# A state-space layer on one core: projection by whole tiles, the step size put in the decay exponent, and the turned x copied by ScalarE

## The chip, the cores and the metric

The kernel runs on one core of a Trainium2 chip. The metric is device time in microseconds (us). The kernel before took 762.07 us, the median of 3 runs (761.32 to 762.39).

## The reference

A decoder layer on x of 4 sequences by 256 tokens by 256 channels: a state-space mixer with 32 heads, a mixture chosen by token id, and a routed mixture of 16 experts, each followed by an addition and a layer norm. The change touches the mixer alone:

```python
proj = x @ Win.T                       # per head: x 64, z 64, B 128, C 128, dt 1
dt = softplus(dt_raw + dt_bias)
xc = silu(causal_conv(x_ssm, w_x)); Bc, Cc likewise       # 4 taps over time
decay = exp(dt * A)
h = dec_t * h + (dt_t * xc_t) * B_t ;  y = h @ C_t        # scan over 256 tokens
y = y * rsqrt(mean(y * y) + 1e-6) * silu(z);  out = y @ Wout.T
```

The kernel has no scan over h. With cum the running sum of dt*A, it takes for each head and sequence y[t] = sum over s <= t of (B_s . C_t) * exp(cum_t - cum_s) * dt_s * xc_s, which is matrix work.

## The kernel before, in words

The heads go in 16 pairs. A pair's projection has six tiles of 128 output channels (x of both heads, B and C of the first head, B and C of the second, z) by 1024 tokens. Everything is pipelined over steps: in step n, `front` is the projection and convolution of pair n, `mid` is the scores of pair q = n-1, `tail` is the end of pair r = n-2. `steps` (L197) runs step 0 (front), step 1 (front, mid), a loop with steps 2 to 15 (all three), step 16 (mid, tail) and step 17 (tail). Each engine has its own hand-written order of a step, and semaphores tie them together. The parts and the short names that the prediction uses:

- TensorE, `step` at L529. P0 to P11 are `project(j)` (L540): j // 2 is the tile, j % 2 the half of the tokens; six matmuls of 128x512 each (two halves of the channels by three products of split operands). P(j) writes PSUM bank j % 4, so it waits until VectorE has done the last tap of the same half two tiles earlier (`half_read`, L211). X0 and X1 are `x_to_tokens` (L532, four transposes each, into banks 4 and 5). S0 to S7 are `score(k)` (L556: sequence k // 2, head k % 2), into bank 4 + k % 2; S(k) waits until W(k-2) has emptied its bank, S0 and S1 until the turned x has been taken from it. M0 to M3 are `mix(p, b)` (L569), one for each sequence, into banks 6 and 7. MS0 and MS1 are `mean_square` (L585).
- Order on TensorE before: P0, M2, M3, MS0, X0, P1, X1, P2, P3, S0, P4, S1, MS1, P5, S2, P6, S3, P7, S4, P8, M0, M1, P9, S5 and so on: one unit of the score behind each projection group. M2, M3, MS0 and MS1 are pair r's, the rest of M, X and S pair q's.
- ScalarE, `step` at L857: z of pair q, then for j = 0 to 9 `copy(j)` (L871: PSUM to `conv`, scaled by the last tap's weight) and what `work[j]` lists: `silu` of tile 4, `square`, a table load (L914), `exp_decay(b)` (L880, the exponential for two units of decay), `rsqrt`; then a table load (L928) and `silu` of tiles 0 to 3.
- VectorE, `step` at L1077: `tap(m, i)` (L1096) adds the three other taps of tile m in place, with half taps and full taps by `TAPS_OF` (L33). t1, t2, t3a, t3b name the taps with shift 1, 2, 3 (first half), 3 (second half); each waits for the one that it builds on. Tile 0 is done in six half taps, tiles 1 to 4 in t1 (full), t2 (full), t3a, t3b. `between` places the other work among them: x_scaled (L1080, the turned x times dt, from banks 4 and 5 to `xs`), W0 to W7 = `weigh(k)` (L1089, score times decay), and `gate` (L1113).
- GpSimd, `step` at L375: `log_decay` (L346: cum_t - cum_s and the mask), `low_part` (L370, needed by MS), the split of the next weights (L335), `norm` (L362).
- SyncE (L230) loads weights two steps ahead and stores and rereads the running sum (L247 to L251).
- Once, within and behind step 0: ScalarE's softplus (L842), VectorE's `sum_dt` (L1053), TensorE's `turn_dt` (L505, 16 small transposes of dt and cum), VectorE's `take_dt` (L1070), for which TensorE and GpSimd wait.

The placing on VectorE before:

```python
between[0, 3] = [lambda: x_scaled(0)]
between[0, 5] = [lambda: x_scaled(1)]
for k, at_ in enumerate(((1, 0), (2, 0), (2, 1), (3, 0), (3, 1), (4, 0), (4, 1), (4, 3))):
    between[at_] = [lambda k=k: weigh(k)]
between[4, 2] = [lambda: gate(q, qp, 0)]
```

Of the kernel before, what the change touches and what calls it, by code (L numbers as in the profile page):

```python
# [15 lines left out]
ALU = mybir.AluOpType  # L16
# [3 lines left out]
P = 128  # L20
NB, T, D = 4, 256, 256
NT = NB * T
TB = NT // P
# [8 lines left out]

TAPS_OF = [[(slice(h, h + 1), s) for h in (0, 1) for s in (1, 2, 3)] if m == 0 else  # L33
           [(slice(0, 2), 1), (slice(0, 2), 2), (slice(0, 1), 3), (slice(1, 2), 3)] for m in range(NCONV)]
TAP_AT = [sum(len(t) for t in TAPS_OF[:m]) for m in range(NCONV + 1)]
# [18 lines left out]
PAD = -3.0e38  # L54
HIT = 3.0e38
LN_EPS = 1e-5
RMS_EPS = 1e-6


def build_layer(nc, xT, x, winT, wdtT, a_log, dt_bias, woutT, ids, ctxT, gateT, ebias, wsh, wgu, wdn, out):  # L60
# [4 lines left out]
    with ExitStack() as ctx:  # L65
# [16 lines left out]
        cum_b = sb("cum_b", [P, 2, 2, NT])  # L82
        dt_tok = sb("dt_tok", [P, TB, H])
        cum_tok = sb("cum_tok", [P, TB, H])
# [59 lines left out]
        def take(n):  # L144
# [31 lines left out]
                 "w_split u_done p_arg p_lo s_done xt_done y_done ms_done "  # L176
                 "a_copy a_z a_silu a_decay a_sq a_ln a_rs "
                 "v_tap v_xs v_m v_yz v_y "
                 "ld_wo ld_xt ld_late ld_rt ln_st "
# [51 lines left out]
        def _(sp):  # L231
# [14 lines left out]
            load_pair(1, 1)  # L246
            sp.wait_ge(S["d_dt"], 3)  # L247
            sp.dma_start(cum_dram, dt_cum).then_inc(S["st_cum"], 16)
# [16 lines left out]
            sp.wait_ge(S["s_done"], NPAIR * UNITS)  # L265
            sp.wait_ge(S["v_xs"], 2 * NPAIR)
            sp.wait_ge(S["xt_done"], 2 * NPAIR)
# [41 lines left out]
        def _(pool):  # L309
# [65 lines left out]
            def step(n, par, split_next, mid, tail, ahead):  # L375

                if mid:
                    log_decay(n - 1, 1 - par, 2)
                if tail:
                    low_part(n - 2, 1)  # L380
                if mid:
                    log_decay(n - 1, 1 - par, 3)
                if split_next:
                    split(n + 1, 1 - par)
                if tail:
                    norm(n - 2, par, 0)
                    norm(n - 2, par, 1)
                if mid:
                    low_part(n - 1, 0)
                if ahead:  # L390
                    log_decay(n, par, 0)
                    log_decay(n, par, 1)
# [102 lines left out]
        def _(pe):  # L495
# [9 lines left out]
            def turn_dt():  # L505

                pe.wait_ge(S["d_dt"], 3)
                pe.wait_ge(S["z_const"], 10)
                for i, src in enumerate((dt_l, dt_cum)):
                    for b in range(TB):  # L510
                        mm = pe.transpose(ps[:, 4 + i, b * H:(b + 1) * H], src[:, b * P:(b + 1) * P],
                                          ident[0:H, 0:H])
                mm.then_inc(S["s_dtT"], 1)
                pe.wait_ge(S["d_dtT"], 1)
# [14 lines left out]
            def step(n, par, front, mid, tail):  # L529
# [26 lines left out]
                def score(k):  # L556
                    b, h = k // 2, k % 2
                    c0, c1 = cols[b]
                    Bm, Cm = conv[:, qp, 1 + 2 * h, :], conv[:, qp, 2 + 2 * h, :]
                    ge(pe, S["a_silu"], q * NCONV + 3 + 2 * h)  # L560
                    if k < 2:
                        ge(pe, S["v_xs"], q * 2 + k + 1)
                    else:
                        ge(pe, S["v_m"], q * UNITS + k - 1)
                    pe.matmul(ps[:, 4 + k % 2, 0:T], Bm[:, c0:c0 + P], Cm[:, c0:c0 + T], start=True, stop=True)  # L565
                    pe.matmul(ps[:, 4 + k % 2, T:SC], Bm[:, c1:c1 + P], Cm[:, c1:c1 + P], start=True, stop=True  # L566
                              ).then_inc(S["s_done"], 1)

                def mix(p, b):  # L569
# [3 lines left out]
                    if b % 2 == 0:  # L573
                        ge(pe, S["v_xs"], p * 2 + 1 + g)
                        ge(pe, S["a_ln"], p * 2 - 1 + g)
# [16 lines left out]
                if front:  # L592
                    ge(pe, S["w_split"], n * 2 + 2)
                    if isinstance(n, int) and n == 0:
                        pe.wait_ge(S["d_x"], 2)
                for j in range(2 * NTILE):
                    if front:
                        project(j)
                    if tail and j == 0:
                        mix(r, 2)  # L600
                        mix(r, 3)
                        mean_square(r, 0)
                        if isinstance(n, int) and n == NPAIR + 1:
                            pe.wait_ge(S["a_z"], 2 * NPAIR)
                            out_project(0, 0, NPAIR - 1)
                    if mid and j < 2:
                        x_to_tokens(j)
                    if mid and 3 <= j < 3 + UNITS:
                        score(j - 3)
                    if mid and j == 8:  # L610
                        mix(q, 0)
                        mix(q, 1)
                    if tail and j == 4:
                        mean_square(r, 1)
# [218 lines left out]
        def _(act):  # L833
# [8 lines left out]
            def softplus(i):  # L842
# [10 lines left out]
                else:  # L853
                    act.wait_ge(S["a_dt"], 4)
                    act.activation(dt_ch, dt_e, ACT.Ln, bias=1.0).then_inc(S["a_dt"], 1)

            def step(n, par, front, mid, tail):  # L857
                q, qp, r = n - 1, 1 - par, n - 2
# [12 lines left out]
                def copy(j):  # L871
                    tile, hf = j // 2, j % 2
                    ge(act, S["u_done"], n * 12 + j + 1)
                    if j == 0 and not (isinstance(n, int) and n < 2):
                        ge(act, S["s_done"], n * UNITS - UNITS)
                    tap = KD * PW + tile * TAPS + TAPS - 1
                    act.activation(conv[:, par, tile, hf * 512:(hf + 1) * 512], ps[:, j % 4, :], ACT.Copy,  # L877
                                   scale=w_raw[:, par, tap:tap + 1]).then_inc(S["a_copy"], 1)

                def exp_decay(b):  # L880
# [24 lines left out]
                if isinstance(n, int) and n == 0:  # L905
                    work[0] += [lambda: softplus(0)]
                    work[1] += [lambda: softplus(1), lambda: softplus(2)]
                    work[2] += [lambda: softplus(3)]
                if mid:
                    work[0] += [lambda: silu(q, qp, 4)]  # L910
                if tail:
                    work[1] += [lambda: square(r, 1)]
                if mid or tail:
                    work[1] += [lambda: act.preload_act_table_set("natural_log_exp_and_others")]  # L914
                if mid:
                    for b, j in enumerate((2, 4, 6, 8)):
                        work[j] += [lambda b=b: exp_decay(b)]
                    work[8].append(lambda: square(q, 0))
                if tail:
                    work[3] += [lambda: rsqrt(r, 0)]  # L920
                    work[6] += [lambda: rsqrt(r, 1)]
                for j in range(2 * NTILE):
# [121 lines left out]
        def _(dve):  # L1044
# [8 lines left out]
            def sum_dt():  # L1053
# [8 lines left out]
                dve.wait_ge(S["a_dt"], 5)  # L1062
                link(dve.tensor_tensor(dt_l, dt_l, dt_ch, ALU.add))
                link(dve.tensor_scalar(dt_da, dt_l, head_c[:, 2:3], -1.0, ALU.mult, ALU.mult))
                for b in range(NB):
                    t = slice(b * T, (b + 1) * T)
                    ins = dve.tensor_tensor_scan(dt_cum[:, t], one[:, :].broadcast_to([H, T]), dt_da[:, t], 0.0, ALU.mult, ALU.add)
                link(ins)

            def take_dt():  # L1070
                dve.wait_ge(S["s_dtT"], 1)
                dve.tensor_copy(dt_tok[:, :, :], ps[:, 4, 0:TB * H].rearrange("p (b h) -> p b h", b=TB))
                dve.tensor_copy(cum_tok[:, :, :], ps[:, 5, 0:TB * H].rearrange("p (b h) -> p b h", b=TB)  # L1073
                                ).then_inc(S["d_dtT"], 1)
                dve.wait_ge(S["d_dtT"], 1)

            def step(n, par, front, mid, tail):  # L1077
                q, qp, r, rp = n - 1, 1 - par, n - 2, par

                def x_scaled(c):  # L1080

                    ge(dve, S["xt_done"], q * 2 + c + 1)
                    ge(dve, S["y_done"], q * UNITS)
                    dve.tensor_tensor(xs[:, 4 * c:4 * c + 4, :].rearrange("p b (h c) -> p b h c", h=2),  # L1084
                                      ps[:, 4 + c, :].rearrange("p (b h c) -> p b h c", b=4, h=2),
                                      dt_tok[:, 4 * c:4 * c + 4, bass.ds(q * 2, 2)].unsqueeze(3)
                                      .broadcast_to([P, 4, 2, HP]), ALU.mult).then_inc(S["v_xs"], 1)

# [33 lines left out]
                if mid:  # L1122
                    between[0, 3] = [lambda: x_scaled(0)]
                    between[0, 5] = [lambda: x_scaled(1)]
                    for k, at_ in enumerate(((1, 0), (2, 0), (2, 1), (3, 0), (3, 1), (4, 0), (4, 1), (4, 3))):
                        between[at_] = [lambda k=k: weigh(k)]
                    between[4, 2] = [lambda: gate(q, qp, 0)]
                if tail:
                    between[0, 4] = [lambda: gate(r, rp, 1)]
                if isinstance(n, int) and n == 0:  # L1130
                    between[1, 0] = [sum_dt]
                for m in range(NCONV):
                    for i in range(len(TAPS_OF[m])):
                        for f in between.get((m, i), []):
                            f()
                        if front:
                            tap(m, i)
            steps(dve, step, take_dt)

# [252 lines left out]
```

## Time and profile before

| what | value |
|---|---|
| median of 3 runs | 762.07 us |
| profiled execution | 762.01 us |
| its span | 760.3 us (1.7 us lie around it) |
| TensorE matmul busy | 676.9 us, 89% |
| VectorE busy | 522.8 us, 69% |
| GpSimd busy | 437.8 us, 58% |
| ScalarE busy | 430.1 us, 57% |

The mixer takes about the first two thirds of the span: step 1 begins at 41.78 us, the steps of the loop at 68.74 us and then every 29.12 us, step 16 at 475.77 us. Busy time counts instructions from start to end and lets neighbours overlap, so an engine can be the bound with less than 100%. The profile is best read as the order of one step of the loop on each engine, since the steps repeat to a few hundredths of a microsecond.

### The profile page before, as it was taken

The numbers are of one execution on the slowest core, as the hardware profiler recorded it, in microseconds if no ns is written. First come the engines' busy times: TensorE is split into PE (matmuls) and PEld (weight loads), VectorE is DVE, ScalarE is ACT, GpSimd is POOL, SyncE is SP. The second block draws the span as 40 slices with busy tenths as digits, with TensorE's granted clock in tenths as the row PEclk, the third lists the DMA queues.
The fourth block names the chain that finished last, engine by engine and source line by source line (L and its number), as shares of the span: only waits on it lengthen the run. The fifth ranks groups of instructions, "written<-read, shape, count | busy, mean of one in ns | idle before, by whom it ended". The sixth has DMA issues, their size and how long they took to land.

```text
span 760.3 us, 11331 instructions
## 1 busy us (share of the span) xinstructions
PE 676.9 (89%) x3376; PEld 521.3 (69%) x3376; DVE 522.8 (69%) x803; ACT 430.1 (57%) x701; POOL 437.8 (58%) x382
## 2 busy tenths in 40 slices
PE   6599999999999999999999999899999986999930
PEld 3477777777777777777777777688846864677720
DVE  5988988988989989989889889512337343222236
ACT  4366777787787687687777777721011242333321
POOL 4076887787787777878868864754000014733134
PEclk9899999999999999999999999999999998999975
DMA  3221121121111211211211200430092401333324
GB/s 141 117 87 54 56 98 42 55 86 50 57 51 61 81 42 57 95 42 55 97 42 55 97 0 0 141 110 1 1 339 75 111 21 28 93 99 99 79 72 128
DMA packets 19968, 57.41 MB, mean 76 GB/s; under 512 B 2998, under 2 KB 13110, under 8 KB 17206
## 3 DMA queue, kind: packets, MB, share of 16 engines
q1 hardware_dynamic: 17686, 50.92, 19.6%
q0 software_dynamic: 2256, 6.16, 3.3%
q8 instruction: 14, 0.23, 0.1%
q14 instruction: 12, 0.10, 0.0%
HBM read 50.78 MB, written 6.29 MB: 75 GB/s over the span
## 4 chain that ended last, share of the span: by engine, by line
PE 51%; DVE 23%; issue 12%; ACT 9%; POOL 2%; DMA 1%; DVEq 1%; ACTq 0%; SPq 0%; POOLq 0%
DVE conv L1109 18%; PE ps L551 13%; PE ps L524 7%; PE ps L579 6%; PE ps L745 5%; PE ps L671 4%; PE ps L645 4%; PE ps L785 4%; ACT conv L877 3%; DVE decay L1093 2%; POOL conv L489 2%; ACT decay L883 2%; ACT y_hi L888 1%; PE ps L763 1%; PE ps L565 1%
## 5 line engine op out<-in xcount | busy, mean ns | idle before, releaser
L1109 DVE SCALAR_TENSOR_TENSOR conv<-ps,w_raw,conv 128x506 f32<-128x506 f32 (+3 forms) x352 | 324.6, 935 | 48.2 <-ACT conv L877 44.6
L551 PE MATMUL ps<-x_hi,w_hi 128*128 128x512 f32 x384 | 166.1, 433 | 29.8 <-DVE conv L1109 27.2
L877 ACT ACTIVATE conv<-ps,w_raw 128x512 f32<-128x512 f32 x160 | 109.3, 684 | 109.4 <-PE ps L551 109.2
L551 PE MATMUL ps<-x_hi,w_lo 128*128 128x512 f32 x384 | 151.6, 395 | 0.0
L551 PE MATMUL ps<-x_lo,w_hi 128*128 128x512 f32 x384 | 151.1, 393 | 0.0
L353 POOL TENSOR_TENSOR decay<-cum_b,cum_tok 128x512 f32<-128x512 f32 (+1 forms) x128 | 103.3, 829 | 35.5 <-DVE cum_tok L1073 23.8
L551 PEld LDWEIGHTS ps<-x_hi,w_hi 128*128 128x128 f32 x384 | 72.7, 189 | 56.2 <-DVE conv L1109 41.7
L373 POOL TENSOR_TENSOR y_lo<-y_sq,y_hi 128x512 fp32r<-128x512 f32 x32 | 41.3, 1289 | 80.1 <-ACT y_sq L889 80.1
L359 POOL TENSOR_TENSOR decay<-decay,mask 128x512 f32<-128x512 f32 x64 | 82.7, 1292 | 5.0
L551 PEld LDWEIGHTS ps<-x_hi,w_lo 128*128 128x128 f32 x384 | 72.5, 189 | 16.8
L551 PEld LDWEIGHTS ps<-x_lo,w_hi 128*128 128x128 f32 x384 | 73.0, 190 | 10.1
L862 ACT ACTIVATE conv<-conv 128x1024 f32<-128x1024 f32 x80 | 79.4, 1049 | 0.2
L565 PE MATMUL ps<-conv 128*128 128x256 f32 x256 | 76.4, 380 | 2.0 <-DVE xs L1084 1.6
L1093 DVE TENSOR_TENSOR decay<-ps,decay 128x384 f32<-128x384 f32 x128 | 70.2, 549 | 7.4 <-ACT decay L883 4.9
L937 ACT ACTIVATE ln_v<-ln_m,eps_ln 128x1 f32<-128x1 f32 x24 | 7.1, 295 | 90.6 <-DVE ln_m L1159 90.6
L524 PE MATMUL ps<-late,y_all 128*128 128x256 f32 x256 | 56.7, 379 | 0.2 <-DVE xs L1148 0.2
L565 PEld LDWEIGHTS ps<-conv 128*128 128x128 f32 x256 | 47.5, 188 | 13.2 <-issue 2.5
L458 POOL DMA_INDIRECT xb<-x_scratch,y_all x31 | 30.0, 967 | 42.5 <-PE ps L721 37.5
L343 POOL TENSOR_TENSOR w_lo<-w_raw,w_hi 128x1536 fp32r<-128x1536 f32 x15 | 53.0, 3531 | 1.2
L883 ACT ACTIVATE decay<-decay 128x768 f32<-128x768 f32 x64 | 53.4, 836 | 0.0
L566 PEld LDWEIGHTS ps<-conv 128*128 128x128 f32 x256 | 48.5, 190 | 6.7
L524 PEld LDWEIGHTS ps<-late,y_all 128*128 128x128 f32 x256 | 48.2, 190 | 6.9 <-DVE xs L1148 0.6
(166 smaller groups left out, 1027.1 us busy)
## 6 DMA issues: line engine op xcount, KB each, us to landing
cum_b<-cum_scratch SPq DMA_DIRECT2D x16, 1024.0 KB, 4.7
w_raw<-in_winT SPq DMA_DIRECT2D x16, 778.0 KB, 4.4
y_all<-in_wgu SPq DMA_DIRECT2D x4, 1408.0 KB, 10.7
ys_scratch<-y_blk SPq DMA_DIRECT2D x31, 128.0 KB, 1.7
late<-in_wdn SPq DMA_DIRECT2D x2, 1408.0 KB
late<-in_woutT SPq DMA_DIRECT2D x1, 2048.0 KB, 8.2
y_all<-in_xT SPq DMA_DIRECT2D x1, 1024.0 KB, 4.9
conv<-in_x SPq DMA_DIRECT2D x1, 1024.0 KB, 5.5
```

What stands on the lines that cost most here:

```text
L343: pool.tensor_tensor(w_lo[:, par, :], raw, w_hi[:, par, :].bitcast(F32), ALU.subtract).then_inc(S["w_split"], 1)
L353: pool.tensor_tensor(decay[:, 2 * b:2 * b + 2, c:t], cum_b[:, qp, :, b * T + j * P:(b + 1) * T], cum_tok[:, 2 * b + j, bass.ds(q * 2, 2)]. ...
L359: pool.tensor_tensor(diag, diag, mask[:, :].unsqueeze(1).unsqueeze(1).broadcast_to([P, 2, 2, P]), ALU.add).then_inc(S["p_arg"], 1)
L524: mm = pe.matmul(ps[:, b % 2, 0:D], y_all[:, i, b * P:(b + 1) * P], wo_sb[:, i, :], start=(i == 0), stop=(i == NPAIR - 1))
L551: mm = pe.matmul(ps[:, j % 4, :], wp[:, par, w], xp[:, kk, t], start=(i == 0), stop=(i == 5))
L565: pe.matmul(ps[:, 4 + k % 2, 0:T], Bm[:, c0:c0 + P], Cm[:, c0:c0 + T], start=True, stop=True)
L566: pe.matmul(ps[:, 4 + k % 2, T:SC], Bm[:, c1:c1 + P], Cm[:, c1:c1 + P], start=True, stop=True).then_inc(S["s_done"], 1)
L862: act.activation(conv[:, pp, tile, :], conv[:, pp, tile, :], ACT.Silu).then_inc(S["a_silu"], 1)
L877: act.activation(conv[:, par, tile, hf * 512:(hf + 1) * 512], ps[:, j % 4, :], ACT.Copy, scale=w_raw[:, par, tap:tap + 1]).then_inc(S["a_c ...
L883: act.activation(d, d, ACT.Exp).then_inc(S["a_decay"], 1)
L1093: dve.tensor_tensor(decay[:, k, :], ps[:, 4 + k % 2, 0:SC], decay[:, k, :], ALU.mult).then_inc(S["v_m"], 1)
L1109: dve.scalar_tensor_tensor(out=o[:, :, s:], in0=u[:, :, 0:T - s], scalar=w_raw[:, par, c:c + 1], in1=o[:, :, s:], op0=ALU.mult, op1=ALU.ad ...
```

## The change

The step size moves into the exponent: exp(cum_t - cum_s) * dt_s becomes exp(cum_t - (cum_s - log dt_s)). Only the second term, cum - log dt, is turned to the token side; dt isn't. The turned x is then copied unscaled by ScalarE instead of multiplied by VectorE. Three small operations are added in step 0 (a maximum and a subtraction on VectorE, a logarithm on ScalarE). The orders of all four engines change with it.

```diff
-TAPS_OF = [[(slice(h, h + 1), s) for h in (0, 1) for s in (1, 2, 3)] if m == 0 else
-           [(slice(0, 2), 1), (slice(0, 2), 2), (slice(0, 1), 3), (slice(1, 2), 3)] for m in range(NCONV)]
+TAPS_OF = [[(slice(0, 2), 1), (slice(0, 2), 2), (slice(0, 1), 3), (slice(1, 2), 3)] for m in range(NCONV)]
...
-            sp.wait_ge(S["d_dt"], 3)
+            sp.wait_ge(S["d_dt"], 4)
...
-            sp.wait_ge(S["v_xs"], 2 * NPAIR)
+            sp.wait_ge(S["a_xs"], 2 * NPAIR)
...
                 if mid:
                     log_decay(n - 1, 1 - par, 2)
+                    log_decay(n - 1, 1 - par, 3)
                 if tail:
                     low_part(n - 2, 1)
-                if mid:
-                    log_decay(n - 1, 1 - par, 3)
...
-                pe.wait_ge(S["d_dt"], 3)
+                pe.wait_ge(S["d_dt"], 5)
                 pe.wait_ge(S["z_const"], 10)
-                for i, src in enumerate((dt_l, dt_cum)):
-                    for b in range(TB):
-                        mm = pe.transpose(ps[:, 4 + i, b * H:(b + 1) * H], src[:, b * P:(b + 1) * P],
-                                          ident[0:H, 0:H])
+                for b in range(TB):
+                    mm = pe.transpose(ps[:, 4, b * H:(b + 1) * H], dt_ch[:, b * P:(b + 1) * P], ident[0:H, 0:H])
...
-                for j in range(2 * NTILE):
+                for tile in range(NTILE):
                     if front:
-                        project(j)
-                    if tail and j == 0:
+                        project(2 * tile)
+                        project(2 * tile + 1)
+                    if tail and tile == 0:
                         mix(r, 2)
                         mix(r, 3)
                         mean_square(r, 0)
...
-                    if mid and j < 2:
-                        x_to_tokens(j)
-                    if mid and 3 <= j < 3 + UNITS:
-                        score(j - 3)
-                    if mid and j == 8:
+                    if mid and tile == 0:
+                        x_to_tokens(0)
+                        x_to_tokens(1)
+                    if mid and tile == 4:
                         mix(q, 0)
                         mix(q, 1)
-                    if tail and j == 4:
+                    if mid and 1 <= tile < 5:
+                        score(2 * tile - 2)
+                        score(2 * tile - 1)
+                    if tail and tile == 2:
                         mean_square(r, 1)
...
+            def log_dt():
+
+                act.wait_ge(S["d_dt"], 2)
+                act.activation(dt_ch, dt_e, ACT.Ln).then_inc(S["a_dt"], 1)
+
...
+                def take_x(c):
+                    ge(act, S["xt_done"], q * 2 + c + 1)
+                    ge(act, S["y_done"], q * UNITS)
+                    act.activation(xs[:, 4 * c:4 * c + 4, :], ps[:, 4 + c, :].rearrange("p (b c) -> p b c", b=4), ACT.Copy
+                                   ).then_inc(S["a_xs"], 1)
+
...
+                    work[4] += [log_dt]
                 if mid:
                     work[0] += [lambda: silu(q, qp, 4)]
-                if tail:
-                    work[1] += [lambda: square(r, 1)]
                 if mid or tail:
                     work[1] += [lambda: act.preload_act_table_set("natural_log_exp_and_others")]
                 if mid:
+                    work[2] += [lambda: take_x(0), lambda: take_x(1)]
+                if tail:
+                    work[3] += [lambda: square(r, 1), lambda: rsqrt(r, 0)]
+                if mid:
                     for b, j in enumerate((2, 4, 6, 8)):
                         work[j] += [lambda b=b: exp_decay(b)]
-                    work[8].append(lambda: square(q, 0))
+                    work[9].append(lambda: square(q, 0))
                 if tail:
-                    work[3] += [lambda: rsqrt(r, 0)]
-                    work[6] += [lambda: rsqrt(r, 1)]
+                    work[7] += [lambda: rsqrt(r, 1)]
...
                 link(dve.tensor_tensor(dt_l, dt_l, dt_ch, ALU.add))
+                link(dve.tensor_scalar(dt_e, dt_l, DT_MIN, None, ALU.max))
...
+            def less_log_dt():
+
+                dve.wait_ge(S["a_dt"], 6)
+                dve.tensor_tensor(dt_ch, dt_cum, dt_ch, ALU.subtract).then_inc(S["d_dt"], 1)
+
...
-                dve.tensor_copy(dt_tok[:, :, :], ps[:, 4, 0:TB * H].rearrange("p (b h) -> p b h", b=TB))
-                dve.tensor_copy(cum_tok[:, :, :], ps[:, 5, 0:TB * H].rearrange("p (b h) -> p b h", b=TB)
+                dve.tensor_copy(cum_tok[:, :, :], ps[:, 4, 0:TB * H].rearrange("p (b h) -> p b h", b=TB)
...
-                    between[0, 3] = [lambda: x_scaled(0)]
-                    between[0, 5] = [lambda: x_scaled(1)]
-                    for k, at_ in enumerate(((1, 0), (2, 0), (2, 1), (3, 0), (3, 1), (4, 0), (4, 1), (4, 3))):
-                        between[at_] = [lambda k=k: weigh(k)]
-                    between[4, 2] = [lambda: gate(q, qp, 0)]
+                    for m in (2, 3, 4):
+                        between[m, 0] = [lambda m=m: weigh(2 * m - 4), lambda m=m: weigh(2 * m - 3)]
+                    between[4, 3] = [lambda: weigh(6)]
                 if tail:
-                    between[0, 4] = [lambda: gate(r, rp, 1)]
+                    between[1, 2] = [lambda: gate(r, rp, 1)]
                 if isinstance(n, int) and n == 0:
                     between[1, 0] = [sum_dt]
+                    between[3, 1] = [less_log_dt]
...
+                if mid:
+                    weigh(7)
+                    gate(q, qp, 0)
```

`S["v_xs"]` is replaced by `S["a_xs"]` in the waits of S0, S1 and `mix`, and the tile `dt_tok` is gone.

## Rows read from the trace of the kernel before

**Rows 1.** Waits within one step of the loop: us in total, times, longest.

```profile
POOL y_lo L373 <- ACT y_sq L889: 5.1, 2, 3.4
...
PE ps L551 <- DVE conv L1109: 2.2, 3, 0.9
```

**Rows 2.** Timeline of TensorE, one step (start us, us, what, idle before).

```profile
243.62 0.50 PE L551 MATMUL ps<-x_hi,w_hi 128*128 128x512 f32 x1 [0.91 <-DVE conv L1109]
...
245.19 1.52 PE L579 MATMUL ps<-decay,xs 128*64 128x256 f32 x16
246.64 0.50 PE L588 MATMUL ps<-y_hi,mean_w 128*128 128x512 f32 x1
...
247.20 0.60 PE L536 MATMUL ps<-ident,conv 128*128 128x128 f32 x4
247.56 0.48 PE L551 MATMUL ps<-x_hi,w_hi 128*128 128x512 f32 x1
...
249.03 0.60 PE L536 MATMUL ps<-ident,conv 128*128 128x128 f32 x4
...
250.86 0.39 PE L551 MATMUL ps<-x_hi,w_hi 128*128 128x512 f32 x1
...
252.22 0.59 PE L565 MATMUL ps<-conv 128*128 128x256 f32 x2
...
252.79 0.47 PE L551 MATMUL ps<-x_hi,w_hi 128*128 128x512 f32 x1
...
272.75 0.50 PE L551 MATMUL ps<-x_hi,w_hi 128*128 128x512 f32 x1 [0.91 <-DVE conv L1109]
```

**Rows 3.** Timeline of ScalarE, the same step.

```profile
244.48 1.06 ACT L868 ACTIVATE z_gate<-ps 128x512 f32<-128x512 f32 x2
...
249.23 0.69 ACT L877 ACTIVATE conv<-ps,w_raw 128x512 f32<-128x512 f32 x1 [2.17 <-PE ps L551]
...
252.79 0.84 ACT L883 ACTIVATE decay<-decay 128x768 f32<-128x768 f32 x1
253.53 0.68 ACT L877 ACTIVATE conv<-ps,w_raw 128x512 f32<-128x512 f32 x1
```

**Rows 4.** Timeline of VectorE, the same step.

```profile
254.24 4.03 DVE L1109 SCALAR_TENSOR_TENSOR conv<-ps,w_raw,conv 128x1020 f32<-128x1020 f32 x4
258.19 0.55 DVE L1093 TENSOR_TENSOR decay<-ps,decay 128x384 f32<-128x384 f32 x1
258.65 1.27 DVE L1109 SCALAR_TENSOR_TENSOR conv<-ps,w_raw,conv 128x1020 f32<-128x1020 f32 x1
...
271.36 0.68 DVE L1117 TENSOR_TENSOR z_gate<-ps,z_gate 128x512 f32<-128x512 f32 x1
271.95 0.74 DVE L1109 SCALAR_TENSOR_TENSOR conv<-ps,w_raw,conv 128x506 f32<-128x506 f32 x1
```

**Rows 5.** Timeline of TensorE in step 16, where two scores follow each other.

```profile
485.46 0.67 PE L565 MATMUL ps<-conv 128*128 128x256 f32 x2 [0.43 <-DVE decay L1093]
...
486.18 0.60 PE L565 MATMUL ps<-conv 128*128 128x256 f32 x2
```

**Rows 6.** Timelines of VectorE and TensorE in and behind step 0.

```profile
19.74 1.21 DVE L1063 TENSOR_TENSOR y_all<-y_all 32x1024 f32<-32x1024 f32 x1 [0.63 <-ACT y_all L855]
20.99 0.74 DVE L1064 TENSOR_SCALAR y_all<-y_all,head_c 32x1024 f32<-32x1024 f32 x1
...
41.31 0.42 DVE L1073 COPY cum_tok<-ps 128x256 f32<-128x256 f32 x1
```

```profile
27.65 0.79 PE L551 MATMUL ps<-x_hi,w_hi 128*128 128x512 f32 x1 [6.84 <-DVE conv L1109]
```

**Rows 7.** Busy us (x instructions) of PE, PEld, DVE, ACT, POOL; clock; DMA; GB/s, by stretch.

```profile
27.60:31.20 3.60, 3.55 (x8) 2.81 (x9) 3.53 (x4) 0.58 (x1) 0.00 (x0) 0.50 0.99 416
...
626.20:630.00 3.80, 0.09 (x1) 0.00 (x0) 3.80 (x4) 0.56 (x2) 3.79 (x3) 0.82 0.02 4
630.00:632.00 2.00, 1.75 (x17) 1.35 (x18) 1.97 (x4) 0.00 (x0) 0.00 (x0) 0.50 0.00 0
```

More of the change, by code:

```diff
@@ L55 @@
 HIT = 3.0e38
+DT_MIN = 1.0e-30
 LN_EPS = 1e-5
@@ L82, in build_layer @@
         cum_b = sb("cum_b", [P, 2, 2, NT])
-        dt_tok = sb("dt_tok", [P, TB, H])
         cum_tok = sb("cum_tok", [P, TB, H])
@@ L176, in build_layer @@
                  "w_split u_done p_arg p_lo s_done xt_done y_done ms_done "
-                 "a_copy a_z a_silu a_decay a_sq a_ln a_rs "
-                 "v_tap v_xs v_m v_yz v_y "
+                 "a_copy a_z a_silu a_xs a_decay a_sq a_ln a_rs "
+                 "v_tap v_m v_yz v_y "
                  "ld_wo ld_xt ld_late ld_rt ln_st "
@@ L561, in score @@
                     if k < 2:
-                        ge(pe, S["v_xs"], q * 2 + k + 1)
+                        ge(pe, S["a_xs"], q * 2 + k + 1)
                     else:
@@ L573, in mix @@
                     if b % 2 == 0:
-                        ge(pe, S["v_xs"], p * 2 + 1 + g)
+                        ge(pe, S["a_xs"], p * 2 + 1 + g)
                         ge(pe, S["a_ln"], p * 2 - 1 + g)
@@ L1078, in step @@
                 q, qp, r, rp = n - 1, 1 - par, n - 2, par
[L1080 to L1087, printed above, removed]
                 def weigh(k):
```

## The prediction

> **What bounds it now.** The timeline of one step of the loop decides, since 14 of the 18 steps repeat it. From P0 to the next P0 it takes 272.75 - 243.62 = 29.13 us [rows 2]. TensorE works nearly throughout. The reader sees only three waits in it, all for VectorE's taps, 2.2 us together and the longest 0.9 us, at P0 [rows 1]. So TensorE would need some 27.0 us alone, and the rest is VectorE not having emptied a bank. VectorE in turn idles only at the head of the step, where it waits for ScalarE's copies; from t1 of tile 1 at 254.24 on [rows 4] it runs nearly without a gap to the t3a that lets P0 go (start 271.95, 0.74 long, end 272.69, P0 at 272.75, so a hand-over costs 0.06). Two cycles are thus nearly equal, and what counts is the order, not the busy sums.
>
> **The prices.** From start to start, TensorE: a projection group behind another one 252.22 - 250.86 = 1.36, behind something else 249.03 - 247.56 = 1.47; a mix pair 1.45 with 0.09 ahead of it; MS 0.56; X 0.36; a score 252.79 - 252.22 = 0.57 [rows 2]. New is a score straight behind another: the first then costs 486.18 - 485.46 = 0.72 [rows 5]. ScalarE: a copy starts 249.23 - 247.56 = 1.67 after its projection group did, 0.57 before what follows it; the exponential takes 0.74; copy start to tap start is 254.24 - 253.53 = 0.71 [rows 2 to 4]. VectorE: t1, t2, t3a, t3b in a row, 258.19 - 254.24 = 3.95, of which t1 and t2 cost 1.32 each since the next tap waits for their end (without that, 1.27 less an overlap of 0.09: 1.18); W 0.46, ended after 0.55; gate 0.59 [rows 4].
>
> **take_x** has no row of its own. Above: the copies with a scale, 0.57 apart. Below: the silu of z, the same size from PSUM without a per-partition operand, (1.06 - 0.58) = 0.48 apart [rows 3]. It is nearest to the latter; I take 0.49, and 0.57 for the upper end (+0.16 a step).
>
> **One step of the new order,** P0 at 0. TensorE: P0, P1 (2 x 1.36), mix pair (0.09 + 1.45), MS0 0.56, X0 and X1 0.72: P2 at 5.54. Its copy starts at 7.21. On ScalarE both take_x and an exponential now stand between copy(2) and copy(3): 0.57 + 2 x 0.49 + 0.74, so copy(3) goes at 9.50, though P3's result is there by 5.54 + 1.47 + 1.36 + 0.2 = 8.6, and t1 of tile 1 starts at 10.21. Before it was 254.24 - 243.62 = 10.62; so 0.4 us is gained here, in spite of the copies. (All that VectorE saves in tile 0, two x_scaled and two half taps made full ones, lies ahead of this point and only makes its idle time longer. I give it nothing. Its cover is that P2 comes late; if P2 came early it would be worth up to 1.5 us.)
>
> Tile 1 on VectorE with the gate in it: 3.95 + 0.59 - 0.14 = 4.40, W0 at 14.61. And here is the new wait. S2 stands behind P5, and needs W0, which now stands behind all taps of tile 1. TensorE has ended S0, S1, P4 and P5 by 5.54 + 2.83 + 1.29 + 2.83 = 12.5 and sits idle until 14.61 + 0.55 + 0.06 = 15.22, **2.7 us**, with P6 and P7 queued behind, which have long been free to go. Before, P5 stood ahead of S2 as well, but W0 stood ahead of tile 1, and P6 followed at once.
>
> From there: S2 0.72, S3 0.57, MS1 0.56, P6 and P7 2.72 give 19.79; W2 starts at 14.61 + 0.92 + 3.95 = 19.48 and frees S4 at 20.09 (0.3 idle); S4, S5 1.29; P8, P9 2.83; mix pair 1.54; S6, S7 1.29; P10, P11 2.83: **next P0 at 29.87**. VectorE's own chain gives t1 of tile 1 + 4.40 + two times 4.87 (pair of W and tile) + 0.92 + 1.32 + 1.32 + 0.74 + 0.06 = 28.7, or 29.0 with a wait for copy(7), and so is no longer last. So a step costs 29.87 - 29.13 = +0.75, **+10.5 us** for 14 steps. The three old waits, 2.2, are indeed gone; 3.0 of new ones stand in their place.
>
> **What is hidden.** ScalarE: square of pair q moves behind copy(9) and the mix pair, so its silus at the step's end and copy(0) come about 1.5 later (copy(0) before at 244.48 + 0.95 - 243.62 = 1.8 [rows 2, 3]); this only eats VectorE's idle time, because copy(2) at 7.21 waits for P2. The cover is thin: by the same walk the table load ahead of copy(2) ends only some 0.4 before it. If that is gone, each 0.1 us costs 0.1 a step. GpSimd: low_part(r, 1) is moved behind one more log_decay, but GpSimd waited 5.1 us a step for the two squares [rows 1], and MS1 now needs it only at 16.5. SyncE's store of the sum comes about 1.2 us later, well ahead of GpSimd, which waits for take_dt anyway. MS1, S6, S7 find their inputs ready.
>
> **Outside the loop.** Step 0: the maximum costs 0.78 (as the scaling, 0.74 long, and the 0.04 by which such linked operations lie apart, 20.99 - 19.74 - 1.21), the later t1 of tile 0 0.4, and less_log_dt 1.21 less 0.2 of hidden tap wait [rows 6]; VectorE is the chain here. Gone is one copy of 0.42 that overlapped its neighbour (the other, cum_tok, stays). Sum +1.8, bounds 1 and 2.5. The eight transposes gone lie beside the taps. Step 1 without a tail, walked alike: +0.4. Step 16 has no P0, so the 0.9 wait ahead of P0 that is in the old 29.13 was never paid there, and the new step has none to save: +0.9. Step 16 itself: S2 waits for gate(r, 1), which now comes behind take_x and exp: +1.5, an estimate, between 0 and 3. **Sum: 1.8 + 0.4 + 10.5 + 0.9 + 1.5 = 15.1**, on 762.0 of the profiled execution (the median of the runs is the same to 0.1): 777. Bounds: prices off by 0.3 us a step either way (take_x, hand-over of W to S, scores in pairs) are 4 us, the rest 3.
>
> **Rivals.**
> (a) *TensorE becomes the bound, faster.* Its sum without waits is 27.0 as before, so 14 x 2.2 are to be had, less the 4.6 outside: 736. It decides at W0: its start would have to be by 12.0, so t1 of tile 1 by 7.6, a microsecond before P3's result exists. For it speaks that VectorE's work falls by a good microsecond a step, and that all three old waits are for it. Against it the order of W0 and S2. 0.09.
> (b) *VectorE's chain stays last.* If scores in pairs and the hand-overs cost less, or TensorE's end of step is quicker, the step is 28.7 to 29.2: with the parts outside 761 to 768. 0.15, a good half of it within 0.2% of before.
> (c) *The clock falls.* The granted clock was 0.50 after TensorE's pause of 6.84 us [rows 6, 7] and after one of 3.8 us (0.82 in it, 0.50 behind) [rows 7]; in the loop with pauses up to 0.9 it held. The new pause is 2.7 us in every step, between the two. At 0.50, which is 1.2 GHz, 8 matmuls took 3.6 us, against 1.8: +1.7 a step if it falls in each, 777 + 24 = 801. The Trainium skill ("TensorE: Matmul & The Clock Gate", its table of advice) warns of idle gaps between bursts of matmuls in just this way; the rows agree for the long pauses and show nothing of one of 2.7. 0.08.
> (d) *It does not do what it says:* the copies on ScalarE delay nothing and copy(3) goes at 8.6 as if alone. Then t1 of tile 1 is 0.9 earlier, the step 29.0, the time 765. Within (b).
>
> **Numbers.** As walked 0.68 (770 to 785), (a) 0.09, (b) and (d) 0.15, (c) 0.08. The likeliest is 777. The range 764 to 788 takes in the first and most of (b), leaves out (a) and (c). Faster by over 0.2% (about what a measurement can tell, 1.5 us) 0.10, within it 0.08, slower 0.82.
>
> **What would show it.** In the step's timeline: S2's pair idle 2 to 3 us until W0, S4 a few tenths, no wait at P0, P6, P8; copy(3) behind two take_x of about 0.6 long and an exponential; step near 29.9. VectorE's idle before t1 of tile 0 grown to 4 us. I am wrong if S2 doesn't wait, if the step is under 29.1, or if the clock in the loop is under 1.00.

## The result, and the profile after

The changed kernel took 791.72 us (median of 4 runs, 790.65 to 794.89) against 762.22 before: a ratio of 1.0396, with a 95% interval of 1.0366 to 1.0427. It is slower by 29.5 us, where 15 were forecast. The profiled execution took 794.89 us with a span of 793.2; it is the longest of the four (mean granted clock 0.945, the others 0.954 to 0.956).

The busy part of its page:

```profile
PE 691.3 (87%) x3368; PEld 530.3 (67%) x3368; DVE 501.5 (63%) x740; ACT 443.5 (56%) x734; POOL 437.6 (55%) x382
```

VectorE's busy time fell by 21 us, as it should, and TensorE's rose by 14 although it does a few transposes less. In the trace of before a matmul of 128x512 takes 0.39 us in a row of them, 0.50 straight behind a pause [rows 2] and 0.79 at half clock [rows 6], so this line points at pauses or at the clock. The length of the steps points at the clock. Timeline of TensorE, the eight transposes (X0, X1) of four steps in a row (start us, us, what):

```profile
232.36 1.03 PE L532 MATMUL ps<-ident,conv 128*128 128x128 f32 x8
...
262.40 0.93 PE L532 MATMUL ps<-ident,conv 128*128 128x128 f32 x7
...
293.81 0.93 PE L532 MATMUL ps<-ident,conv 128*128 128x128 f32 x7
...
323.86 0.93 PE L532 MATMUL ps<-ident,conv 128*128 128x128 f32 x7
```

The steps alternate: 30.04, 31.41, 30.05 us, and so on over the whole loop; before, every step took 29.1 us [rows 2]. Waits in the long step that P0 begins at 257.58 (us in total, times, longest):

```profile
ACT conv L881 <- PE ps L547: 7.5, 3, 6.1
DVE conv L1117 <- ACT conv L881: 7.0, 3, 4.2
...
PE ps L561 <- DVE decay L1101: 2.4, 1, 2.4
```

The waits of TensorE for taps [rows 1] are gone. One for a weighing stands in their place, ahead of S2, and VectorE idles 4.2 us at the head of the step (3.8 in the short one before it). The timeline of TensorE shows S2 of two steps, with its pause:

```profile
242.84 0.70 PE L561 MATMUL ps<-conv 128*128 128x256 f32 x2 [2.38 <-DVE decay L1101]
...
272.88 1.10 PE L561 MATMUL ps<-conv 128*128 128x256 f32 x2 [2.39 <-DVE decay L1101]
```

Both pauses are 2.4 us, but behind the second the same two matmuls take 1.10 us instead of 0.70. The stretches behind the two pauses, and one at the start of step 1 and one in step 16 (busy us of PE, PEld, DVE, ACT, POOL, then granted clock, DMA share, GB/s):

```profile
242.80:246.00 3.20, 3.16 (x16) 2.77 (x17) 3.13 (x4) 0.00 (x0) 3.12 (x2) 1.00 0.00 0
272.80:276.30 3.50, 3.42 (x10) 2.91 (x11) 3.43 (x5) 0.00 (x0) 3.42 (x2) 0.54 0.00 0
44.07:47.40 3.33, 3.33 (x8) 2.61 (x9) 0.00 (x0) 0.58 (x1) 3.17 (x4) 0.54 0.68 222
509.60:518.70 9.10, 8.54 (x24) 7.06 (x25) 3.23 (x6) 6.55 (x11) 6.69 (x7) 0.50 0.20 62
```

At 2.4 GHz behind the one, near 1.2 GHz behind the other. So the added time of the loop is made of two things: a step that is 0.9 us longer at the full clock, and half clock behind the pause in every second step (steps 2, 4 and so on to 14), 1.35 us each.

**Where the 32.9 us of the profiled execution lie**, by equal points of both traces: 2.3 up to P0 of step 1 (44.07 against 41.78 us); 2.3 in step 1; 22.3 from there to X0 of step 16, of which seven steps with half clock are 9.3; 4.9 from X0 of step 16 to the first transposes of the output projection, where S0 waits 3.1 us for ScalarE and the clock is 0.50 behind it; 1.1 after that, which was not followed further. What half clock cost in steps 1 and 16 can be read from later runs. Experiments 7 (with 6) and 8 have the same order in step 1; the first had half clock at its start and took 26.70 us for it, the other had none and took 25.30: 1.4 of the 2.3. In step 16 the profiles of experiment 2 (even) and experiment 3 have the changed kernel's order, a pause of 2.8 us and granted clock 1.00 throughout, and they take 2.6 us less from X0 on, of which 0.3 is the shorter pause: 2.3 of the 4.9. Half clock is then some 13 us in all, and the rest, some 20 us, is the order at the full clock.

### The profile page after: what moved, and what is told of

It reads as the page before. It is cut to its first block, busy times and chain, and to the rows that moved or that the text cites. A ratio compares the mean times of both kernels' runs of the same rounds, so it can differ in the third digit from the quotient of the medians.

```text
span 793.2 us, 11229 instructions
## 1 busy us (share of the span) xinstructions
PE 691.3 (87%) x3368; PEld 530.3 (67%) x3368; DVE 501.5 (63%) x740; ACT 443.5 (56%) x734; POOL 437.6 (55%) x382
## 4 chain that ended last, share of the span: by engine, by line
PE 47%; issue 16%; DVE 15%; POOL 14%; ACT 6%; DMA 1%; POOLq 1%; DVEq 1%; SPq 0%; ACTq 0%
PE ps L547 10%; DVE conv L1117 9%; POOL decay L352 9%; PE ps L520 7%; PE ps L744 5%; PE ps L561 4%; PE ps L670 4%; PE ps L644 3%; PE ps L784 3%; PE ps L575 2%; DVE decay L1101 2%; PE ps L562 2%; ACT conv L881 2%; POOL conv L487 1%; POOL decay L358 1%
## 5 line engine op out<-in xcount | busy, mean ns | idle before, releaser
L1117 DVE SCALAR_TENSOR_TENSOR conv<-ps,w_raw,conv 128x1020 f32<-128x1020 f32 (+1 forms) x320 | 316.9, 1008 | 101.5 <-ACT conv L881 96.3
L547 PE MATMUL ps<-x_hi,w_hi 128*128 128x512 f32 x384 | 158.3, 412 | 11.4 <-DVE conv L1117 10.1
L561 PE MATMUL ps<-conv 128*128 128x256 f32 x256 | 90.7, 440 | 40.2 <-DVE decay L1101 36.6
L547 PEld LDWEIGHTS ps<-x_hi,w_hi 128*128 128x128 f32 x384 | 74.4, 194 | 27.2 <-DVE conv L1117 11.3
L367 POOL TENSOR_TENSOR y_all<-z_gate,y_all 128x512 f32 (+1 forms) x32 | 41.5, 1296 | 54.0 <-ACT y_all L906 54.0
L1101 DVE TENSOR_TENSOR decay<-ps,decay 128x384 f32<-128x384 f32 x128 | 66.3, 548 | 6.1 <-PE ps L562 6.0
L562 PE MATMUL ps<-conv 128*128 128x128 f32 x256 | 54.0, 296 | 0.0
L456 POOL DMA_INDIRECT xb<-x_scratch,y_all x31 | 30.1, 970 | 42.6 <-PE ps L720 37.6
```

Source lines behind the costliest of these rows:

```text
L367: pool.tensor_tensor(dst, z_gate[:, pp, h], y_rs[:, g, :], ALU.mult).then_inc(S["v_y"], 1)
L547: mm = pe.matmul(ps[:, j % 4, :], wp[:, par, w], xp[:, kk, t], start=(i == 0), stop=(i == 5))
L1101: dve.tensor_tensor(decay[:, k, :], ps[:, 4 + k % 2, 0:SC], decay[:, k, :], ALU.mult).then_inc(S["v_m"], 1)
L1117: dve.scalar_tensor_tensor(out=o[:, :, s:], in0=u[:, :, 0:T - s], scalar=w_raw[:, par, c:c + 1], in1=o[:, :, s:], op0=ALU.mult, op1=ALU.ad ...
```

## The experiments

Ratios are to the kernel before, run on the same chip in the same rounds; where microseconds of two jobs are compared, the ratio times 762.2 is used. The step lengths are from the profiles.

**1. The pause filled.** P5 is computed twice in each step with scores (same operands, same bank, same result; only the second tells the others that it is done).

```diff
                         project(2 * tile)
+                        if mid and 2 * tile + 1 in (5,):
+                            project(2 * tile + 1, filler=True)
                         project(2 * tile + 1)
```

> The changed kernel, with P5 computed twice in every step that has scores: six more matmuls of 1.37 us in the pause before S2, same result. Theory one (the clock): in the changed kernel steps alternate between 30.05 and 31.4 us because the granted clock falls after every second pause of 2.4 us. With the pause cut to about 1.1 us the clock stays at 1.00, every step takes 30.05, and the whole is some 10 to 12 us faster than the changed kernel, 780 to 783 us, although TensorE does more. Theory two (the long steps come from a wait that varies with the order of the loop's two steps, and the clock only follows it): steps go on alternating, and the time stays at 791 us. Theory three (TensorE itself is short of time): 1.37 us more a step, 810 us.

Measured: 781.20 us, ratio 1.0217 (1.0189 to 1.0246). Its timeline of TensorE and the stretch behind the pause:

```profile
257.82 1.04 PE L532 MATMUL ps<-ident,conv 128*128 128x128 f32 x8
...
268.30 0.70 PE L562 MATMUL ps<-conv 128*128 128x256 f32 x2 [1.03 <-DVE decay L1104]
...
287.89 1.04 PE L532 MATMUL ps<-ident,conv 128*128 128x128 f32 x8
```

```profile
268.30:271.80 3.50, 3.50 (x18) 3.03 (x19) 3.43 (x4) 0.05 (x1) 3.42 (x2) 1.00 0.00 0
```

Every step of the loop takes 30.02 to 30.07 us, with 1.4 us more matmul work in it. Theory one holds. By the ratios, 0.018 x 762 = 13.6 us of the 30 come from the pauses' effect on the clock (10.5 us by the medians of the two jobs), and 1.0217, some 779 us, is the time of the change's order without it. (In step 16 its profile still has half clock: 0.56 from 499.6 to 507.4 us.)

**2. The filler in one half of the steps.** As before, but only in even steps (`par == 0`), and only in odd ones.

> The changed kernel with P5 computed twice only in the even steps, those whose pause was followed by half clock in its profile. Theory one (a pause of 2.4 us can bring the clock down in any step; which one is a matter of when it falls): the odd steps' pauses stay at 2.4 us, and some of them may now be followed by half clock: anything from 781 to 791 us, with long steps among the odd ones if any. Theory two (something in the even steps themselves, as the buffer half or the loop's turn, makes them long): all steps 30.05, 781 us.

> The same with P5 twice only in the odd steps, those that kept the clock. Theory one: the even steps' pauses are still there, and at least half of them are followed by half clock, 785 to 791 us. Theory two (what makes the even steps long is independent of the odd ones): 791 us, every even step 31.4, exactly as in the changed kernel.

Measured: even 789.51 us, 1.0329 (1.0284 to 1.0374); odd 792.33 us, 1.0379 (1.0322 to 1.0437). In the profile with even steps filled, the even steps take 30.04, and of the seven odd ones, which had kept their clock in the changed kernel, four (3, 5, 7 and 9) now take 31.3, and the last (15) has half clock behind its pause too (0.60 from 484.3 to 488.6). Stretches behind an unfilled and a filled pause of it:

```profile
241.40:245.00 3.60, 3.58 (x13) 3.02 (x14) 3.53 (x4) 0.00 (x0) 3.52 (x3) 0.69 0.00 0
272.70:276.00 3.30, 3.25 (x17) 2.82 (x17) 3.23 (x4) 0.00 (x0) 3.22 (x2) 1.00 0.00 0
```

With odd steps filled the even ones take 31.3 to 31.4, as in the changed kernel. That second run alone would also fit its theory two; it is the first run, and experiment 3, where the long steps are all odd, that rule out something in the even steps themselves. The same pause of 2.4 us is followed by half clock at one time and not at another, and in the changed kernel it is every second one; what decides which one was not found. Filling half of them did not protect the others.

**3. A shorter pause.** Only two of P5's six matmuls doubled.

> The changed kernel with only two of P5's matmuls doubled, 0.46 us more work in the pause: about 1.9 us instead of 2.4. The pauses seen so far: none of 1.0 or 1.7 us in every step was followed by half clock, those of 2.0 and 2.4 us in every second step. If the length decides and the bound lies near 2: 781 to 787 us, with fewer long steps than 7 or none. If it doesn't: 791 us.

Measured: 789.83 us, 1.0333 (1.0287 to 1.0378), an interval that overlaps the changed kernel's (1.0366 to 1.0427). The pause is 1.94 us, and seven of them are still followed by half clock, now in the odd steps 3 to 15. The last of the seven, the stretch behind it, and step 16, whose pause of 2.8 us was followed by none:

```profile
487.08 0.70 PE L564 MATMUL ps<-conv 128*128 128x256 f32 x2 [1.93 <-DVE decay L1106]
```

```profile
487.00:491.00 4.00, 3.92 (x13) 3.30 (x14) 3.93 (x6) 0.00 (x0) 0.00 (x0) 0.59 0.00 0
506.50:520.00 13.50, 8.60 (x57) 6.91 (x58) 4.80 (x9) 11.51 (x17) 11.08 (x11) 1.00 0.35 115
```

The first branch of the expectation missed: 0.46 us off the pause removed no long step, and 2 us is not a bound that one can stay just under.

**4. A control of the filler**, in the version of experiment 7, which has no pause there.

> A control: the same filler (P5 twice, in every step with scores) in the version with the weighings in their own tiles and the first exponential behind copy(3), where no pause stands ahead of S2. Theory one (the filler helps only where it fills a pause; here TensorE is the bound): the step goes from 27.53 to 28.9 us, the whole from 743.8 to 762 to 765 us. Theory two (more matmuls by themselves keep the clock up and pay for themselves): at or under 750 us.

Measured: 757.97 us, 0.992 (0.9891 to 0.9948), against 0.9719 without the filler; the step goes from 27.53 to 28.47. Theory one holds in kind, but its numbers (28.9 us, 762 to 765 us) were too high: the filler costs 0.94 us a step where there is no pause to fill, not the whole 1.37. Without it TensorE's weight loads wait 0.7 us a step for VectorE, and with it they don't; this may be the difference, but was not tried apart. The filler has no merit of its own.

**5. W0 and W1 alone into tile 1.**

```diff
-                    for m in (2, 3, 4):
+                    between[1, 1] = [lambda: weigh(0)]
+                    between[1, 2] = [lambda: weigh(1)]
+                    for m in (3, 4):
...
-                    between[1, 2] = [lambda: gate(r, rp, 1)]
+                    between.setdefault((1, 2), []).append(lambda: gate(r, rp, 1))
```

> The changed kernel with only W0 and W1 moved, from ahead of tile 2 into tile 1, between its taps. Theory one (each pair of scores waits for the pair of weighings behind the tile before): the pause before S2 is gone, but S4 then stands waiting for W2, which is still behind tile 2, for about 2.3 us: the wait moves by one tile, the step is 29.8 to 30.1, the clock still falls now and then, 783 to 792 us. Theory two (S2's pause is all that is wrong): the step is 27.5 to 28.5 us, the clock holds, 745 to 760 us.

Measured: 792.57 us, 1.0352 (1.0313 to 1.0391). S2 waits no longer, S4 does:

```profile
241.91 0.70 PE L561 MATMUL ps<-conv 128*128 128x256 f32 x2 [0.16 <-DVE decay L1101]
248.20 0.70 PE L561 MATMUL ps<-conv 128*128 128x256 f32 x2 [2.02 <-DVE decay L1101]
```

The steps are 29.9 and 31.5 in turn. Theory one: the wait went on to the next tile, and behind every second one of these waits of 2.0 us the clock is down as before (the time is 0.6 us above the range given).

**6. All three pairs into their own tiles.**

```diff
-                    for m in (2, 3, 4):
-                        between[m, 0] = [lambda m=m: weigh(2 * m - 4), lambda m=m: weigh(2 * m - 3)]
+                    for m in (1, 2, 3):
+                        between[m, 1] = [lambda m=m: weigh(2 * m - 2)]
+                        between[m, 2] = [lambda m=m: weigh(2 * m - 1)]
```

The gate at (1, 2) stays there, behind W1, as in experiment 5.

> The changed kernel with the first three pairs of weighings each inside its own tile, between t1 and t2 and between t2 and t3a, where they also fill the time in which a tap waits for the one before. Theory one: no score waits more than 0.5 us for a weighing, the next step's P0 waits for t3a of tile 4 as in the kernel before, the step is 28.1 us (walked by the same prices: t1 of tile 1 at 10.3, W2 at 16.6, t3a of tile 4 ends at 28.0), the clock stays at 1.00, and the whole is about 751 us, faster than both kernels. Theory two (grouping the projection by tiles costs of itself, by coarser hand-overs of banks): the step stays at or above 29.1 us, 765 us or more.

Measured: 754.55 us, 0.987 (0.9841 to 0.9898), step 28.26 us (28.1 expected). Its matmuls wait at most 0.3 us for a weighing. The largest entry for TensorE and a weighing in one step of it is of the weight loads:

```profile
PEld ps L561 <- DVE decay L1101: 0.8, 2, 0.5
```

This version differs from the changed kernel by where six instructions of VectorE stand, and by nothing else, and is 5% faster: some 14 us are the clock (experiment 1) and the rest, some 26, is the shorter step. The wait for t3a at P0, which the expectation had, did not come back. The projection by whole tiles is not at fault.

**7. The first exponential behind copy(3)**, alone and with experiment 6.

```diff
+                if mid:
+                    work[3] += [lambda: exp_decay(0)]
                 if tail:
                     work[3] += [lambda: square(r, 1), lambda: rsqrt(r, 0)]
                 if mid:
-                    for b, j in enumerate((2, 4, 6, 8)):
+                    for b, j in ((1, 4), (2, 6), (3, 8)):
```

> The changed kernel with the first exponential moved on ScalarE from ahead of copy(3) to right behind it. Theory one (copy(3) is on the path: P2, copy(2), two take_x, exponential, copy(3), tile 1's taps, W0, S2): everything behind comes 0.74 us earlier, the step is 29.3 us; the pause before S2 shrinks to about 1.7 us and the clock holds, so some 22 us less than the changed kernel, 768 to 772 us. If the clock still falls in every second step: 780 us. Theory two (ScalarE is not on the path, the step is set by TensorE's and VectorE's work): no change from 791 us.

> The weighings in their own tiles and the first exponential behind copy(3), both on the changed kernel. Theory one (two terms that add until TensorE's own work, 27.0 us and a few tenths of hand-overs, is the bound): the step falls from 28.26 to about 27.5, the whole from 754.5 to about 744 us. Theory two (VectorE's chain from the head of the step is what is left in 28.26 and starts from copy(1), not from copy(3)): no change from 754.5 us.

Measured: alone 770.86 us, 1.0102 (1.0064 to 1.014), step 29.33, pause 1.66 us; in its profile no step is long, though its five runs spread from 769.1 to 775.4 with clocks from 0.973 down to 0.959, so a pause of this length may not be quite safe either (no profile of the slower ones was taken). With experiment 6: **743.76 us, 0.9719 (0.9694 to 0.9745)**, step 27.53. Timeline of TensorE of this last one, X0 of two steps, and S2:

```profile
240.96 1.03 PE L532 MATMUL ps<-ident,conv 128*128 128x128 f32 x8
...
248.90 0.59 PE L561 MATMUL ps<-conv 128*128 128x256 f32 x2
...
268.48 1.03 PE L532 MATMUL ps<-ident,conv 128*128 128x128 f32 x8
```

S2, at 248.90, has no pause any more. One ScalarE instruction moved by one place is worth 0.72 and 0.73 us a step in the two settings (30.05 to 29.33, 28.26 to 27.53), nearly the 0.74 that it takes: copy(3) was on the path in both.

**8. Step 16.** As the last one, with take_x ahead of silu and the table load in step 16 alone.

> As the run before it, and in step 16 alone ScalarE takes the turned x ahead of silu of tile 4 and the table load, since no projection gives it time there. Theory one (the pause before S0 in step 16, 2.3 us with the weighings moved, 3.1 us in the changed kernel, is on the path to the output projection and brings the clock down behind it): 2 to 3.5 us less than the run before it. Theory two (the output projection waits for GpSimd's norms anyway): the same within 0.5 us.

Measured: 743.02 us, 0.971 (0.9685 to 0.9735), the same as without it. S0's pause fell from 2.3 us to 0.3; 1.9 us then stand ahead of another score. The pauses only moved. Theory one also had the clock wrong: in the profile without this edit it stayed at 1.00 behind the 2.3 us, and in the profile with it, the longest of its four runs at 745.53, it fell behind the 1.9 (stretch as above):

```profile
463.70:471.40 7.70, 6.88 (x24) 5.20 (x26) 3.14 (x6) 4.95 (x8) 5.26 (x5) 0.56 0.00 1
```

**9. The algebra alone,** on the kernel before: dt in the exponent, both copies by ScalarE behind copy(2), VectorE without x_scaled, all orders else as they were.

```diff
-                    between[0, 3] = [lambda: x_scaled(0)]
-                    between[0, 5] = [lambda: x_scaled(1)]
...
                 if mid:
+                    work[2] += [lambda: take_x(0), lambda: take_x(1)]
                     for b, j in enumerate((2, 4, 6, 8)):
```

> The kernel before with the step size in the exponent and the copies of the turned x by ScalarE (both behind copy(2), as in the changed kernel), and nothing reordered: the six half taps of tile 0, TensorE's order and the placing of the weighings stay. Theory one (VectorE's saving of two x_scaled is idle time, ScalarE's two copies are ahead of copy(3)): t1 of tile 1 comes 1.0 us later, the step is 30.1 us, with the 2.2 us at the start some 777 to 781 us. Theory two (VectorE is the bound and its 1.2 us a step are gained): 745 to 750 us. Theory three (the two cancel): 763 us.

Measured: 780.84 us, 1.0198 (1.0167 to 1.023), step 30.1. From its timelines, ScalarE's copies and VectorE's first weighing with its wait:

```profile
262.24 1.08 ACT L886 ACTIVATE xs<-ps 128x512 f32<-128x512 f32 x2
263.19 0.85 ACT L892 ACTIVATE decay<-decay 128x768 f32<-128x768 f32 x1
263.93 0.70 ACT L880 ACTIVATE conv<-ps,w_raw 128x512 f32<-128x512 f32 x1
```

```profile
264.17 0.56 DVE L1100 TENSOR_TENSOR decay<-ps,decay 128x384 f32<-128x384 f32 x1 [1.68 <-ACT decay L892]
```

Taking 1.2 us of work a step off VectorE makes the step 1.0 us longer, because the same work on ScalarE stands ahead of copy(3) and of the exponential that W0 waits for, while what VectorE gained is idle time. t1 of tile 1 starts 11.6 us behind P0 here, 10.6 in the kernel before. In the changed kernel the earlier P2 makes up for this: there it starts 10.3 us behind P0. So the algebra alone loses, by its copies ahead of copy(3). The new order without the algebra was not run.

## Why the prediction was right and wrong

- *The wait of S2 for W0* was forecast at 2.7 us by the trace of before, measured 2.39 (S2 starts 15.30 behind P0, 15.22 forecast; the pause is shorter because TensorE's work ahead of it ended at 12.9 and not at 12.5). Right, and shown as the cause by experiments 5 and 6.
- *The step at full clock*: 29.87 forecast, 30.05 measured. Within it t1 of tile 1 at 10.21 forecast, 10.29 measured (267.87 less 257.58); take_x at 0.49, measured 0.48 (265.45 to 266.40 for the two). The 0.18 missing are the two X in a row (0.79 rather than 0.72) and, behind S4, pairs of scores at 1.33 rather than 1.29; the hand-over from W to S was priced right (W0 at 272.28, S2 at 272.88).
- *The clock.* This is the step that failed. The likeliest case read the loop as running at 1.00, and the rival that says otherwise, (c), had 0.08. The trace of before held pauses of up to 0.9 us in the loop with the clock up and of 3.8 and more with it down, and in the loop nothing between (outside it one of 1.8 us, at 564.2, with the clock at 1.00 behind it); the 2.7 was nearer to the longer end, and a chance near one half was due. Its price was nearly right, 1.7 us forecast for a fall and 1.35 measured (why it is less was not tried apart). It came in half of the steps instead of all. With the order as it was and the pause filled (experiment 1), no step of the loop is long and the time lies inside the range, so it is this step that put the time outside. The warning of the Trainium skill ("TensorE: Matmul & The Clock Gate", its table of advice) against idle gaps between bursts holds here down to about 2 us in a periodic loop (1.94, experiment 3); the page sets its warning at longer gaps than these, and the measurement decides.
- *Outside the loop* 4.6 us were forecast; 10.6 were measured, and that with the 0.9 ahead of step 16 counted in the loop's 22.3. The start was nearly right (1.8 against 2.3). Step 1 (0.4 against 2.3) lost 1.4 to half clock. Step 16 (1.5 against 4.9) lost 2.3 to it, and S0's wait there for the copies was not in the sum. The last 1.1 had no term.
- *The range* 764 to 788 ended 4 us short. Without the clock the sum was 777, and experiment 1 gives 779 for it by its ratio. That the two are so near is partly luck: by the traces the order without half clock costs some 20 us (13 in the loop, 7 elsewhere) where 15.1 were forecast, each term a little short.
- *The rivals.* (a), TensorE as the bound at a faster time, falls for this order, and is nearly what the mended order does: 27.5 a step, with 27.0 forecast as TensorE's own. (d), the exponential and copies off copy(3)'s path, is experiment 7: 0.73 of the 0.9 that it named, and with the W to S wait in place it gives 771, not 765.

## What to carry to other kernels

Ask of each instruction of an engine not what it costs but what stands behind it: six weighings and one exponential, moved by a place or two with no work saved, took this kernel from a ratio of 1.040 to one of 0.972. Here the consumer's result that frees the producer's next buffer belonged inside the consumer's current piece of work and not behind it. It also filled a wait between dependent operations there: in experiment 6 a weighing starts 1.19 us behind t1 (250.42 to 251.61), where t2, which needs the end of t1, started 1.32 behind it in the kernel before (254.24 to 255.56). And where a change makes a pause of TensorE of 2 us or more that comes round in a loop, count the half clock behind it as a likely case, since the trace before can't show it.

## What was not expected of the hardware

- Pauses of 1.94, 2.0 and 2.4 us were followed by half clock in about every second step, and the same pause at another moment was not. Of 1.0 us none was; of 1.66 us none in the profile. Length alone doesn't decide: in step 16 pauses of 2.3 (experiment 7) and 2.8 us (experiments 2, even, and 3) and 3.0 us (experiment 4) were followed by none, in the changed kernel one of 3.1 us was.
- Work made this loop faster by filling a pause: 1.4 us more matmuls a step, 10.5 us less in all.
- In step 16 the granted clock stayed at 0.50 for 9 us, with TensorE busy 8.5 of them on scores and MS1, where in the kernel before the same work ran at 1.00. With the same order and the same pause of 3.1 us in experiment 2 (odd), it was 0.50 only for the first two scores and 1.00 from 512.6 to 519.6 us. What holds it down was not tried apart.
